# Where the first value products of a head and the wait for a later head's operands stand in TensorE's order

## The chip, the cores and the metric

One core of one Trainium2 chip runs the whole program. The metric is the time of one execution on the device, in microseconds (us). Three runs of the kernel before took 1323.6, 1324.37 and 1325.23 us.

## The reference

The program is one macaron block over x of 4 sequences x 1024 tokens x 128 channels in float32: half a mixture of experts, attention, and half a mixture of experts again.

```
x = x + 0.5 * ffn(layernorm(x))
x = x + attn(layernorm(x))      # 16 heads of 8 channels, rotary q and k
x = x + 0.5 * ffn(layernorm(x))

scores  = einsum('bhqd,bhkd->bhqk', q, k) * SCALE      # 1024 x 1024 per head
weights = softmax(scores, axis=-1)
attn    = einsum('bhqk,bhkd->bhqd', weights, v)
```

The change touches the attention only, between q, k, v and the output projection: 4 x 16 = 64 heads of 1024 queries by 1024 keys.

## The kernel before

Each engine has its own instruction stream, written out by hand. The streams meet in counting semaphores. The attention is a pipeline over the 64 heads, called n here: heads 0 to 3 and 60 to 63 are written out, heads 4 to 59 are a hardware loop of 14 rounds of four heads (u = 0 to 3 in a round).

A head has 16 steps on TensorE, i = 0 to 15 (`head`, line 919). A step i issues one score product K(i) of head n (`key_scores`, line 886: 128 keys by 512 queries, with the row maximum already folded in through three extra rows) and one score product M(i) of head n+2 (`max_scores`, line 855: 128 queries by 512 keys, only for the row maximum). K and M use different halves of the array's rows. I call one such step a pair of score products. After every odd step stands a value product W(kb) (`weigh_values`, line 896): eight short matrix products that weigh 128 keys' values by their exponentials. LAG = 2 sets which one: after steps 1 and 3 it is W(6) and W(7) of the head before, after steps 5, 7, ... 15 it is W(0), W(1), ... W(5) of this head. Before step MT_AT = 7 stands T (`max_transpose`, line 877), a product with 24 columns that turns the maximum of head n+1 round; ScalarE copies it (`mrow_copy`) and a DMA puts it into that head's Q.

What waits for what:

- K(i) needs a free score bank of three (`bank_free`, line 869). K(0) waits for exponential E(14) of the head before, K(1) for its E(15), K(6) for E(3), K(7) for E(5), T for E(4).
- M(2t) waits until VectorE has read pair t-2 (`max_read`, line 863), as there are two places for maximum scores. R(t) is VectorE's reduction of M(2t) and M(2t+1) (line 1235). M(6) waits for R(1).
- M(0) waits besides for the operands of head n+2 (`head_loaded`, line 860). SyncE starts these loads for head n+3 at the start of head n (line 352), once W(7) of head n-1 has been issued and done.
- W(0) waits for its exponentials, for `ot_ready` (line 903) and for `vh_ready` (line 904). `ot_ready` comes from ScalarE's copy O of the output bank of the head before (line 649), which stands in ScalarE's stream right behind E(3).
- ScalarE runs E(0) to E(15) in order (line 661), with O behind E(3) and the copy of T ahead of E(7).

Of the kernel before, what the change touches and what calls it, by code (L numbers as in the profile page):

```python
# [46 lines left out]
NH = B * H  # L47
# [11 lines left out]
PIECE = H * CH // P  # L59
QSLOTS = 4  # L60
LAG = 2
PSLOTS = 8
HALVES = 2 * KB

# [11 lines left out]
def at_least(eng, sem, count):  # L76

    if isinstance(count, int) and count <= 0:
        return
    eng.wait_ge(sem, count)  # L80
# [49 lines left out]
def build(nc, x_in, qkv_w, qkv_b, v_b, out_w, out_b, wr_t, w1_in, w2_t, cos_t, sin_t, out):  # L130
# [4 lines left out]
    with ExitStack() as ctx:  # L135
        def sb(name, shape, dt=F32):
            return ctx.enter_context(nc.sbuf_tensor(name, shape, dt))

        def sem(name):
            return ctx.enter_context(nc.semaphore(name))  # L140
# [59 lines left out]
        K = [K_all[u // 2 * HALF:(u // 2 + 1) * HALF, u % 2, :] for u in range(QSLOTS)]  # L200
        probs = sb("probs", [P, PSLOTS, T])

# [76 lines left out]
        head_loaded = [sem(f"head_loaded{u}") for u in range(QSLOTS)]  # L279
# [257 lines left out]
        def _(sc):  # L537
# [113 lines left out]
            def head(r, u, more=True, first=False):  # L651
                n = QSLOTS * r + u
                for i in range(HALVES):
# [4 lines left out]
                    if j == 0:  # L658

                        at_least(sc, probs_used, KB * (n - 1) + kb + 1)  # L660
                    nc.scalar.activation(probs[:, kb % PSLOTS, j * CH:(j + 1) * CH], score[i],  # L661
                                         ACT.Exp, scale=SCALE).then_inc(probs_ready, 1)
# [20 lines left out]
        def _(pe):  # L683
# [5 lines left out]
            def x_transposes(p, k, rotated, bank=tpsum):  # L689
                pe.wait_ge(xn_ready, p + 1)  # L690

                at_least(pe, rot_ready, 2 * rotated)
                at_least(pe, x_lo_ready, p)
                transposes(xn[:, k, :, :], bank).then_inc(xT_in_psum, 1)
# [30 lines left out]
            def values(c):  # L725

                pe.wait_ge(rot_ready, 2 * c + 2)
                for t in range(TPC):
                    last = nc.tensor.matmul(mpsum_all[:, t * P:(t + 1) * P], x2T[:, t * P:(t + 1) * P], wqkv[:, 4, :],  # L729
                                            start=True, stop=True)  # L730
                last.then_inc(v_in_psum, 1)

            def router(p, k, valued, bank=rpsum):
                pe.wait_ge(xnT_ready, p + 1)

                at_least(pe, v_ready, valued)
                at_least(pe, gap_ready, p)
                if isinstance(p, int) and p == 1:

                    pe.wait_ge(w_lo_ready, E)  # L740
                for t in range(TPC):
                    last = nc.tensor.matmul(bank[:, t, :], xnT[:, k, t * P:(t + 1) * P], wr[:], start=True, stop=True)  # L742
                last.then_inc(logits_in_psum, 1)
# [12 lines left out]
            def out_projection(c, bank=tpsum):  # L756
                pe.wait_ge(attn_ready, c + 1)
                for t in range(TPC):
                    last = nc.tensor.matmul(bank[:, t * P:(t + 1) * P], attn[:, t * P:(t + 1) * P], wo[:], start=True, stop=True)  # L759
                last.then_inc(proj_in_psum, 1)  # L760
# [91 lines left out]
                first_max_scores(t)  # L852
            values(NCH - 1)

            def max_scores(r, u, i):

                t, half = i // 2, i % 2
                n = QSLOTS * r + u
                if i == 0:
                    pe.wait_ge(head_loaded[u], 32 * (r + 1))  # L860
                if half == 0:

                    pe.wait_ge(max_read, KB * n + t - 1)
                last = nc.tensor.matmul(maxps[t % 2][:, half, :], Q[u][0:STACK, t * P:(t + 1) * P],  # L864
                                        K[u][0:STACK, half * CH:(half + 1) * CH], start=True, stop=True)
                if half == 1:
                    last.then_inc(max_in_psum, 1)
# [9 lines left out]
            def max_transpose(r, u, first=False):  # L877

                n = QSLOTS * r + u
                pe.wait_ge(mparts_ready, n + 1)  # L880
                if not first:
                    bank_free(n - 1, MT_AT, True)
                nc.tensor.transpose(mpsum, mparts[:, u % 2, :, :].rearrange("p i t -> p (i t)"),  # L883
                                    identb[:]).then_inc(mT_in_psum, 1)

            def key_scores(r, u, i, row):

                n = QSLOTS * r + u
                kb, j = i // 2, i % 2
                if i == 0:  # L890
                    pe.wait_ge(mrow_loaded[u], 16 * (r + 1))
                bank_free(n, SCORE_PLACE[i], row)
                nc.tensor.matmul(score[i], K[u][0:ROWS, kb * P:(kb + 1) * P],  # L893
                                 Q[u][0:ROWS, j * CH:(j + 1) * CH], start=True, stop=True).then_inc(scores_in_psum, 1)

            def weigh_values(r, u, kb):


                n = QSLOTS * r + u
                pe.wait_ge(probs_ready, HALVES * n + 2 * kb + 2)  # L900
                if kb == 0:

                    at_least(pe, ot_ready, n)
                    pe.wait_ge(vh_ready, n + 1)
                for c in range(QUARTERS):
                    last = nc.tensor.matmul(opsum[VW * c:VW * (c + 1), :], vh[:, u % 2, kb, :],  # L906
                                            probs[:, kb % PSLOTS, c * QW:(c + 1) * QW],
                                            start=(kb == 0), stop=(kb == KB - 1), skip_group_check=True)
                last.then_inc(probs_used, 1)

            pe.wait_ge(max_read, KB)
            for i in range(HALVES):
                if i == MT_AT:
                    max_transpose(0, 0, first=True)
                max_scores(0, 1, i)

            pe.wait_ge(v_ready, NCH)

            def head(r, u, maxes=True, row=True, first=False, early=None):
                for i in range(HALVES):  # L920
                    kb, j = i // 2, i % 2
                    if i == MT_AT and row:
                        max_transpose(r + (u + 1) // QSLOTS, (u + 1) % QSLOTS)
                    key_scores(r, u, i, row)
                    if maxes:
                        max_scores(r + (u + 2) // QSLOTS, (u + 2) % QSLOTS, i)
                    if j == 1 and kb >= LAG:
                        weigh_values(r, u, kb - LAG)
                    elif j == 1 and not first:
                        weigh_values(r + (u - 1) // QSLOTS, (u - 1) % QSLOTS, KB + kb - LAG)  # L930
                    if early == 0 and i == 5:

                        pe.wait_ge(max_read, KB * NH)
                        out_projection(0, early_t)
                    if early == 1 and i == 3:
                        x_transposes(NCH, 0, 0, early_t)
                    if early == 1 and i == 9:
                        router(NCH, 0, 0, early_r)

            for u in range(QSLOTS):  # L940
                head(0, u, first=(u == 0))
            with pe.Fori(1, NH // QSLOTS - 1) as r:
                for u in range(QSLOTS):
                    head(r, u)
            for u in range(QSLOTS):
                head(NH // QSLOTS - 1, u, maxes=u < 2, row=u < 3, early=u - 2)
            for kb in range(KB - LAG, KB):
                weigh_values(NH // QSLOTS - 1, QSLOTS - 1, kb)
            pe.wait_ge(ot_ready, NH)
# [375 lines left out]
```

## Time and profile before

| what | value |
|---|---|
| median of three runs | 1324.37 us |
| the profiled execution | 1324.05 us, its span 1322.1 us |
| attention, heads 0 to 63 | about 385 to 1021 us of the span |
| TensorE busy | 1269.0 us (96%) |
| VectorE busy | 1112.9 us (84%) |
| ScalarE busy | 809.9 us (61%) |
| granted TensorE clock, mean of the span | 0.984 |

The span is from the first to the last instruction; the 1.95 us between it and the execution's time lie around it. Busy shares are means over stages with different limits, so the argument below reads one head of the loop instruction by instruction. The start of a TensorE instruction in a timeline is recorded; its end is modelled, so distances between starts are used.

### The profile page before, as it was taken

To read this page: it belongs to the slowest core of one execution; us is meant where nothing else is said; L and a number is where in the kernel's file an instruction comes from. 1 tells how busy PE (TensorE), PEld (TensorE's weight loads), DVE (VectorE), ACT (ScalarE), POOL (GpSimd) and SP (SyncE) were. 2 spreads that over 40 slices of the span, in tenths; PEclk is the share of its full clock that TensorE was granted. 3 is DMA by queue.
4 is the path that set the end of the run, shared out by engine and by line. 5 is a ranking of instruction groups with operands and counts; after the bars stand their busy time and mean duration, and the time that the engine had idled before them with its cause. 6 is when DMAs were issued, how large, how long until landed. Compare 5 with 4: busy or idle time off the path is not lost.

```text
span 1322.1 us, 32042 instructions
## 1 busy us (share of the span) xinstructions
PE 1269.0 (96%) x10240; PEld 616.0 (47%) x10240; DVE 1112.9 (84%) x2306; ACT 809.9 (61%) x1540; POOL 143.4 (11%) x450
## 2 busy tenths in 40 slices
PE   6999999999889999999999999999999999999998
PEld 3666666667522222222222222222223776767776
DVE  7888867887789999999999999999994787777775
ACT  4433333333239999999999999999997333333332
POOL 1020122111221111111111111111110000000000
PEclk9999999999969999999999999999998999999999
DMA  7010111011211100101101011010010100000000
GB/s 207 1 30 19 49 49 48 12 37 49 67 54 32 42 31 31 40 30 39 32 30 40 31 31 40 30 40 31 31 54 14 35 27 27 27 27 21 13 9 9
DMA packets 52265, 48.49 MB, mean 37 GB/s; under 512 B 10080, under 2 KB 44768, under 8 KB 52192
## 3 DMA queue, kind: packets, MB, share of 16 engines
q1 hardware_dynamic: 52192, 47.61, 12.4%
q8 instruction: 34, 0.56, 0.2%
q14 instruction: 39, 0.32, 0.1%
HBM read 23.86 MB, written 23.33 MB: 36 GB/s over the span
## 4 chain that ended last, share of the span: by engine, by line
PE 89%; DVE 5%; issue 4%; ACT 1%; DVEq 0%; DMA 0%; ACTq 0%; SPq 0%
PE ps L765 23%; PE ps L906 22%; PE ps L893 21%; PE ps L752 16%; PE ps L722 2%; PE ps L864 1%; PE ps L742 1%; DVE X L1092 1%; PE ps L686 1%; PE ps L883 1%; PE ps L729 1%; ACT probs L661 1%; DVE mx L1235 1%; DVE act L1080 1%; PE ps L759 1%
## 5 line engine op out<-in xcount | busy, mean ns | idle before, releaser
L1235 DVE TENSOR_REDUCE mx<-ps 128x1 f32<-128x1024 f32 x512 | 591.7, 1217 | 35.9 <-PE ps L864 30.0
L661 ACT ACTIVATE probs<-ps 128x512 f32<-128x512 f32 x1024 | 562.4, 597 | 60.7 <-PE ps L893 42.6
L590 ACT ACTIVATE sg<-ps,unscale 128x512 f32<-128x512 f32 x256 | 173.8, 687 | 307.2 <-PE ps L765 283.0
L906 PE MATMUL ps<-probs,vh 128*32 128x256 f32 x4096 | 330.7, 395 | 16.9 <-issue 11.5
L893 PE MATMUL ps<-Q,K 51*128 51x512 bf16 x1024 | 333.3, 386 | 0.9 <-ACT probs L661 0.5
L864 PE MATMUL ps<-K,Q 48*128 48x512 bf16 x1008 | 327.1, 389 | 2.9 <-DVE mx L1235 2.5
L752 PEld LDWEIGHTS ps<-w,act 128*128 128x128 f32 x2048 | 247.9, 192 | 17.1
L752 PE MATMUL ps<-w,act 128*128 128x128 f32 x2048 | 249.0, 275 | 0.0
L1080 DVE SCALAR_TENSOR_TENSOR act<-ps,unscale,sg 128x512 f32<-128x512 f32 x256 | 183.3, 744 | 60.0 <-ACT sg L590 19.2
L765 PE MATMUL ps<-x_hi,w_hi 128*128 128x512 f16 x512 | 195.6, 382 | 9.9 <-DVE act L1080 6.4
L1092 DVE SCALAR_TENSOR_TENSOR X<-ps,rw,X 128x128 f32<-128x128 f32 (+1 forms) x512 | 143.9, 343 | 62.4 <-PE ps L752 61.8
L765 PE MATMUL ps<-x_lo,w_hi 128*128 128x512 f16 x512 | 195.4, 382 | 0.0
L765 PE MATMUL ps<-x_hi,w_lo 128*128 128x512 f16 x512 | 195.3, 381 | 0.0
L893 PEld LDWEIGHTS ps<-Q,K 51*128 51x128 bf16 x1024 | 72.7, 93 | 235.4 <-ACT probs L661 227.5
L906 PEld LDWEIGHTS ps<-probs,vh 128*32 128x32 f32 x4096 | 82.8, 108 | 207.8 <-ACT probs L661 162.1
L765 PEld LDWEIGHTS ps<-x_hi,w_hi 128*128 128x128 f16 x512 | 51.8, 101 | 63.9 <-DVE act L1080 12.0
L765 PEld LDWEIGHTS ps<-x_hi,w_lo 128*128 128x128 f16 x512 | 50.4, 98 | 61.4 <-issue 1.7
L864 PEld LDWEIGHTS ps<-K,Q 48*128 48x128 bf16 x1008 | 71.7, 93 | 14.0 <-DVE mx L1235 9.4
L765 PEld LDWEIGHTS ps<-x_lo,w_hi 128*128 128x128 f16 x512 | 50.3, 98 | 49.6 <-issue 5.5
L502 POOL TENSOR_SCALAR negm<-mx 128x8 f32<-128x8 f32 x64 | 15.1, 236 | 493.0 <-DVE mx L1235 493.0
L481 POOL TENSOR_TENSOR qf<-rot 128x512 f32<-128x512 f32 x16 | 20.4, 1274 | 258.9 <-DVE rot L1124 258.9
L580 ACT ACTIVATE tanh_gap<-gap 128x4 f32<-128x4 f32 x16 | 3.3, 204 | 52.5 <-DVE gap L1049 52.5
(84 smaller groups left out, 608.9 us busy)
## 6 DMA issues: line engine op xcount, KB each, us to landing
o_parts<-ot SPq DMA_DIRECT2D x64, 128.0 KB, 1.9
q_stack<-parts SPq DMA_DIRECT2D x48, 128.0 KB, 2.3
k_stack<-parts SPq DMA_DIRECT2D x48, 128.0 KB, 2.3
Q<-q_stack SPq DMA_DIRECT2D x64, 96.0 KB, 2.3
K<-k_stack SPq DMA_DIRECT2D x64, 96.0 KB, 2.3
probs<-w_in SPq DMA_DIRECT2D x8, 256.0 KB, 4.3
att<-o_parts SPq DMA_DIRECT2D x16, 128.0 KB, 2.6
rden<-rdens SPq DMA_DIRECT2D x16, 128.0 KB, 2.5
```

Source lines behind the costliest of these rows:

```text
L481: nc.gpsimd.tensor_tensor(qf[:, w, :], rot[:, w, 0, :], rot[:, w, 1, :], ALU.add).then_inc(rot_sum, 1)
L590: nc.scalar.activation(sg[:, j, :], hid[2 * j], ACT.Silu, scale=unscale[:, e, 2 + j:3 + j]).then_inc(silu_done, 1)
L661: nc.scalar.activation(probs[:, kb % PSLOTS, j * CH:(j + 1) * CH], score[i], ACT.Exp, scale=SCALE).then_inc(probs_ready, 1)
L722: last = nc.tensor.matmul(bank, wqkv[:, 2 * w + i, :], x2T[:], start=True, stop=True)
L752: last = nc.tensor.matmul(ypsum[s][:, t, :], act[:, s, j, t * P:(t + 1) * P], w2[:, e, j, :], start=(j == 0), stop=(j == 1))
L765: last = nc.tensor.matmul(bank, w[:, e, at:at + P], x[:, k, :], start=(n == 0), stop=(n == 2))
L864: last = nc.tensor.matmul(maxps[t % 2][:, half, :], Q[u][0:STACK, t * P:(t + 1) * P], K[u][0:STACK, half * CH:(half + 1) * CH], start=True ...
L893: nc.tensor.matmul(score[i], K[u][0:ROWS, kb * P:(kb + 1) * P], Q[u][0:ROWS, j * CH:(j + 1) * CH], start=True, stop=True).then_inc(scores_ ...
L906: last = nc.tensor.matmul(opsum[VW * c:VW * (c + 1), :], vh[:, u % 2, kb, :], probs[:, kb % PSLOTS, c * QW:(c + 1) * QW], start=(kb == 0), ...
L1080: nc.vector.scalar_tensor_tensor(out=act[:, e % 2, j, :], in0=hid[2 * j + 1], scalar=unscale[:, e, j:j + 1], in1=sg[:, j, :], op0=ALU.mult ...
L1092: last = nc.vector.scalar_tensor_tensor(out=xt, in0=ypsum[e % 2][:, t, :], scalar=rw[:, k, t, e:e + 1], in1=xt, op0=ALU.mult, op1=ALU.add)
L1235: nc.vector.tensor_reduce(mx[:, u % 2, t:t + 1], pair.rearrange("p a b -> p (a b)"), AX_X, ALU.max).then_inc(max_read, 1)
```

## The change

Three things change, all in TensorE's stream.

W(0) is issued after step 6 and no longer after step 5. T, which stays ahead of step 7, then stands right behind it. All other value products stay where they were.

The wait for `head_loaded` leaves M(0). It stands ahead of K(15) of the head before (`operands`, called in `head` at the last step); for the first heads it stands ahead of the maximum scores of head 1 and ahead of head 0.

The order of the out projection (line 934) and of W(0) in head 62 is turned round by the first point.

```diff
+FIRST_VALUES = 2 * LAG + 2
...
+            def operands(r, u):
+                pe.wait_ge(head_loaded[u], 32 * (r + 1))
+
             def max_scores(r, u, i):
...
-                if i == 0:
-                    pe.wait_ge(head_loaded[u], 32 * (r + 1))
...
             pe.wait_ge(max_read, KB)
+            pe.wait_ge(head_loaded[1], 32)
...
-            def head(r, u, maxes=True, row=True, first=False, early=None):
+            operands(0, 2)
+
+            def head(r, u, maxes=True, row=True, first=False, early=None, ahead=True):
                 for i in range(HALVES):
                     kb, j = i // 2, i % 2
+                    if i == HALVES - 1 and ahead:
+                        operands(r + (u + 3) // QSLOTS, (u + 3) % QSLOTS)
...
-                    if j == 1 and kb >= LAG:
+                    if i == FIRST_VALUES:
+                        weigh_values(r, u, 0)
+                    elif j == 1 and kb > LAG:
                         weigh_values(r, u, kb - LAG)
-                    elif j == 1 and not first:
+                    elif j == 1 and kb < LAG and not first:
                         weigh_values(r + (u - 1) // QSLOTS, (u - 1) % QSLOTS, KB + kb - LAG)
...
-                head(NH // QSLOTS - 1, u, maxes=u < 2, row=u < 3, early=u - 2)
+                head(NH // QSLOTS - 1, u, maxes=u < 2, row=u < 3, early=u - 2, ahead=u < 1)
```

## Rows read from the trace of the kernel before

**Rows 1.** The page's costliest groups: busy us, mean ns, idle before, releaser.

```profile
L1235 DVE TENSOR_REDUCE mx<-ps 128x1 f32<-128x1024 f32 x512 | 591.7, 1217 | 35.9 <-PE ps L864 30.0
L906 PE MATMUL ps<-probs,vh 128*32 128x256 f32 x4096 | 330.7, 395 | 16.9 <-issue 11.5
```

**Rows 2.** Busy time of each engine while the loop runs, PE first.

```profile
427.00:975.00 548.00, 531.88 (x5435) 147.72 (x5432) 516.99 (x449) 503.41 (x1009) 70.38 (x336) 1.00 0.11 34
```

**Rows 3.** Timeline of PE (start, us, instruction): K(0) of heads 4 and 60.

```profile
427.11 0.39 PE L893 MATMUL ps<-Q,K 51*128 51x512 bf16 x1
...
975.45 0.37 PE L893 MATMUL ps<-Q,K 51*128 51x512 bf16 x1
```

**Rows 4.** Timeline of PE, steps 13 and 14 of head 21, and W(5) in halves.

```profile
601.34 0.38 PE L893 MATMUL ps<-Q,K 51*128 51x512 bf16 x1
...
601.65 0.64 PE L906 MATMUL ps<-probs,vh 128*32 128x256 f32 x8
602.23 0.39 PE L893 MATMUL ps<-Q,K 51*128 51x512 bf16 x1
...
602.76 0.42 PE L906 MATMUL ps<-probs,vh 128*32 128x256 f32 x4
...
603.00 0.40 PE L906 MATMUL ps<-probs,vh 128*32 128x256 f32 x4
```

**Rows 5.** Timeline of PE, start of head 22: K(0), M(0), K(1).

```profile
603.38 0.39 PE L893 MATMUL ps<-Q,K 51*128 51x512 bf16 x1
603.58 0.38 PE L864 MATMUL ps<-K,Q 48*128 48x512 bf16 x1
603.87 0.39 PE L893 MATMUL ps<-Q,K 51*128 51x512 bf16 x1
```

**Rows 6.** Timeline of ACT: E(15) of head 21.

```profile
603.22 0.59 ACT L661 ACTIVATE probs<-ps 128x512 f32<-128x512 f32 x1
```

**Rows 7.** Timeline of ACT, head 22: E(3), the copy O, E(5).

```profile
605.75 0.59 ACT L661 ACTIVATE probs<-ps 128x512 f32<-128x512 f32 x1
...
606.23 0.39 ACT L649 ACTIVATE ot<-ps 128x256 f32<-128x256 f32 x1
...
606.97 0.63 ACT L661 ACTIVATE probs<-ps 128x512 f32<-128x512 f32 x1
```

**Rows 8.** Timeline of PE, head 22: K(5), W(0), T, K(7).

```profile
606.09 0.38 PE L893 MATMUL ps<-Q,K 51*128 51x512 bf16 x1
...
606.72 0.64 PE L906 MATMUL ps<-probs,vh 128*32 128x256 f32 x8 [0.25 <-issue]
...
607.61 0.23 PE L883 MATMUL ps<-identb,mparts 128*24 128x128 bf16 x1
607.77 0.39 PE L893 MATMUL ps<-Q,K 51*128 51x512 bf16 x1
```

**Rows 9.** Timeline of DVE, head 22: R(1).

```profile
605.47 1.21 DVE L1235 TENSOR_REDUCE mx<-ps 128x1 f32<-128x1024 f32 x1
```

**Rows 10.** Timeline of PE, head 28, first of its round: K(5), W(0).

```profile
664.77 0.38 PE L893 MATMUL ps<-Q,K 51*128 51x512 bf16 x1
...
665.53 0.64 PE L906 MATMUL ps<-probs,vh 128*32 128x256 f32 x8 [0.39 <-ACT ot L649]
```

**Rows 11.** Timelines of DVE and PE ahead of head 0: an R, an M that waits.

```profile
376.80 1.22 DVE L1235 TENSOR_REDUCE mx<-ps 128x1 f32<-128x1024 f32 x1
...
378.08 0.60 PE L864 MATMUL ps<-K,Q 48*128 48x512 bf16 x1 [1.86 <-DVE mx L1235]
```

**Rows 12.** Timeline of PE in the second mixture: two kinds of full-array products.

```profile
1100.44 0.38 PE L765 MATMUL ps<-x_hi,w_lo 128*128 128x512 f16 x1
1100.65 0.61 PE L752 MATMUL ps<-w,act 128*128 128x128 f32 x4
```

**Rows 13.** The operand load: its issue in head 22, and the page's median landing.

```profile
606.60 0.37 SPq L352 DMA_DIRECT2D K<-k_stack  x1
...
K<-k_stack SPq DMA_DIRECT2D x64, 96.0 KB, 2.3
```

## The prediction

> **What bounds the kernel now.** I read the page first, then the busy times of the loop, then the timeline of one head. VectorE's reductions cost most [rows 1] and sat idle only 35.9 us in all, nearly always for a maximum score. So two engines are close to full. While the loop runs, TensorE is busy 531.9 of 548 us, VectorE 517.0, ScalarE 503.4 [rows 2]. A head takes (975.45 - 427.11) / 56 = 9.79 us [rows 3]. The chain of waits follows TensorE, so the timeline of its starts decides.
>
> The unit is two pairs of score products and a value product. The last pair before a value product costs 0.31 us, from 601.34 to 601.65. The value product costs 0.58, from 601.65 to 602.23 (0.57 by the unrounded starts). Its two halves start 0.24 apart [rows 4]. With 0.22 for the other pair a unit is 1.11 us, and eight of them are 8.86. The remaining 0.9 us of a head are three places. At the head's start K(1) comes 0.49 after K(0) where 0.22 would do [rows 5]. W(0) comes 0.63 after K(5) where 0.31 would do [rows 8]. T puts 0.25 between K(6) and K(7). The change touches all three.
>
> **Part 1, the wait for operands.** It is one register calculation and one wait. Today M(0) starts 0.20 after K(0), where K and M otherwise start together [rows 5], so this looks like the cause of the loss at the head's start. It isn't: E(15) of the head before ends at 603.22 + 0.59 = 603.81 [rows 6], and K(1) starts at 603.87, one semaphore later. K(1) may not write its bank sooner, whatever M(0) does. E(15) hangs on E(14) and that on K(14) at 602.23 [rows 4]. So I cost the gain at zero; the cover is E(15), and without it the gain could be 0.49 - 0.22 = 0.27 us a head.
>
> In its new place the wait stands ahead of K(15), M(15) and W(5), and K(0) is queued behind these. Its condition is old by then: the K load is issued at 606.60 and lands some 2.3 us later, at 608.9 [rows 13]; K(15) of this head stands a pair and a value product (0.31 + 0.61) ahead of the next K(0), and so at about 603.38 + 9.79 - 0.92 = 612.2. Slack is over 3 us. The issue cost is bounded below by 0 and above by the 0.20 us that M(0) shows today. Even 0.20 is swallowed: K(1) has 0.27 us in hand against its predecessors on TensorE, and E(15) starts behind E(14), not behind K(15). I take 0. No DMA is moved by it, and SyncE's, GpSimd's and VectorE's orders are untouched.
>
> **Part 2, W(0) one pair later.** Removed: the stall at W(0). O runs from 606.23 to 606.62, behind E(3) [rows 7], and W(0) starts at 606.72 [rows 8], against 606.40 with no wait. That is 0.32 us of idle TensorE in each head. Moving K(6) and M(6) ahead would fill it. K(6) can: E(3) ends at 605.75 + 0.59 = 606.34 [rows 7], so K(6) starts at about 606.40.
>
> What is late next is M(6). It needs R(1), which ends at 605.47 + 1.21 = 606.68 [rows 9]. From an R's end to the waiting M I read 378.08 - 378.02 = 0.06 us [rows 11]. So M(6) can't start before 606.74, about when W(0) starts today. TensorE takes instructions in order: W(0), T, K(7), M(7), then VectorE's R(3), all queue behind M(6). O is past by then. The stall changes its owner from ScalarE's copy to VectorE's reduction, and W(0) moves from 606.72 to 606.74 + 0.31 [rows 4] = 607.05.
>
> Then T. Today it follows K(6) and sits between two changes of the array's shape, each with a gap of about 0.1 us: a 512-column product takes 0.21 us where products of one shape follow each other [rows 12], but 0.31 ahead of a value product [rows 4]. Now it follows W(0). No row of before shows that pair. The upper bound is the 0.57 of a value product before a score product [rows 4]. The lower bound is what lets K(7) start: K(7) needs E(5), which ends at 606.97 + 0.63 = 607.60 [rows 7], so K(7) >= 607.65. I take 0.48, twice the distance of W's halves [rows 4]: T uses all 128 rows and 24 columns, W all rows and 32, and the halves, equal in shape, follow with no such gap.
>
> The Trainium skill, TensorEngine Tiling (Array Packing), Key Properties, says that changing the tiling mode drains the engine while changing only the tile doesn't. That agrees with the gaps above and would give my value if T counts as a 32-column tile.
>
> The row of like shapes [rows 12] shows 0.21 us, hence no time for loading weights between two products on the same rows. The Trainium skill, TensorE: Matmul & The Clock Gate, Part 3, says that a weight load overlaps running products only when the row group differs; by that rule T's load would stand bare behind W(0) and the sum would be that of the first rival. The trace speaks against the rule there.
>
> The sum for one head:
>
> - now K(7) at 607.77 [rows 8];
> - then 606.74 + 0.31 + 0.48 + 0.16 (T to K(7), 607.77 - 607.61 [rows 8]) = 607.69. Gain 0.08 us.
> - In the first head of each round W(0) comes 0.76 after K(5) [rows 10], not 0.63. These 0.13 are extra time at W(0) behind O. M(6) now waits longer than that, so they disappear under its wait. Gain 0.08 + 0.13 = 0.21, with rounding 0.22.
>
> After K(7) all is as before: R(3) comes earlier by the same time, VectorE is busy 517.0 / 56 = 9.23 us of a 9.7 us head [rows 2], and E(14), E(15) hang on K(14), so K(1)'s stall travels along unchanged.
>
> Over the loop: 42 x 0.08 + 14 x 0.22 = 6.4 us. The eight heads outside give about nothing: without loop arithmetic W(0) waits less there, so the exchange is even; head 62 may gain 0.2 by having the projection before W(0). Total 6.6 us. The profiled execution would go from 1324.05 to 1317.5, which stands 0.3 under the median; against the median the forecast is **1317.8 us**. With K(7) at its floor the gain is 42 x 0.12 + 14 x 0.26 = 8.7, so 1315.7.
>
> **The rivals.**
>
> *T pays for the change anyway.* With 0.57 behind W(0), K(7) comes at 607.78. 42 heads lose 0.01, 14 gain 0.12: 1.3 us, with head 62 1.5, so **1322.9 us**, no measurable change. For it: every change of work around W shows the gap [rows 4]. Against it: W's own halves don't.
>
> *Slower: M(6) holds up the instruction stream.* W(0) carries two waits of its own besides that for its exponentials. If they are worked off only once M(6) has gone, W(0) follows not at 0.31 but with the extra 0.13 us that the first head of a round shows at this place [rows 10]. It decides if the issue work behind M(6) exceeds the 0.31 us that M(6) covers, and then the waits of T add theirs, so that T comes at 0.57. K(7) is at 607.78 + 0.14 = 607.92: 42 x 0.15 = 6.3 us lost, the first heads of rounds even: **1330.7 us**. For it: the M(0) that follows K(0) by 0.20 behind such a wait [rows 5]. Against it: weight loads and products stream ahead of running ones elsewhere, and there the register work is covered by a product of 0.3 us.
>
> *The head's start opens after all.* If K(1) hangs on M(0) and not on E(15), 56 x 0.27 = 15 us more go: **1302.7 us**. Against it stand the 0.06 us between E(15)'s end and K(1) [rows 5, 6], which is the usual semaphore time.
>
> *The change doesn't do what it says* would mean that O still is last at W(0). O ends at 606.62 and M(6) can't go before 606.74, so this would take R(1) coming 0.1 us sooner; the time would be that of the floor.
>
> **How the numbers follow.** Forecast with its floor 0.58, T's gap 0.22, held-up stream 0.13, head's start 0.04, the rest 0.03, split over both sides. A measurement of this kernel tells about 0.2%, 2.65 us, from no change. The forecast and the head's start are faster: 0.63 with a part of the rest; T's gap is the same; the held-up stream is slower. The range takes in the floor (1315.7, with a little for reading) and T's gap with an issue cost of 0.03 us a head on top (1324.6), 0.8 of the chance: 1315.4 to 1324.6.
>
> **What the changed profile would show.** K(6) starts ahead of M(6) by some 0.3 us in each loop head, and M(6) is put down to VectorE. W(0) is no longer released by ScalarE's copy. W(0) to T is 0.48 (right) or 0.57 (first rival). M(6) to W(0) is 0.31 (right) or 0.4 and more (second). M(0) starts within 0.1 of K(0), yet K(1) stays 0.49 behind K(0). All four heads of a round take 9.7 us, and ScalarE's E(6) comes 0.3 us sooner with nobody waiting for it. The prediction is wrong above all if W(0) to T is misjudged, since 0.1 us there is 5.6 us of the result, or if R(1) moves against the head's start.

## The result and the profile after

The changed kernel takes 1314.55 us, the median of six runs from 1312.99 to 1315.37; the kernel before, run beside it, 1324.16 (1322.73 to 1325.71). The ratio is 0.9929, its 95% interval 0.9919 to 0.9939. The change is faster by 9.6 us; 6.6 were forecast, and the result lies 0.85 us below the lower end of the range.

| what | before | after |
|---|---|---|
| the profiled execution, us | 1324.05 | 1314.48 |
| its span, us | 1322.1 | 1312.4 |
| loop, K(0) of head 4 to K(0) of head 60 | 548.34 | 540.57 |
| head 0, K(0) to K(0) of head 1 | 13.31 | 11.94 |
| TensorE / VectorE / ScalarE busy, us | 1269.0 / 1112.9 / 809.9 | 1275.5 / 1111.3 / 803.4 |
| granted clock, mean of the span | 0.984 | 0.985 |

The page's costliest groups after the change, to be set against [rows 1]:

```profile
L1243 DVE TENSOR_REDUCE mx<-ps 128x1 f32<-128x1024 f32 x512 | 591.4, 1217 | 27.3 <-PE ps L866 21.3
L908 PE MATMUL ps<-probs,vh 128*32 128x256 f32 x4096 | 329.3, 394 | 0.0
```

VectorE idles 8.6 us less, and no idle time of TensorE is left before the value products (16.9 before). The busy times while the loop runs, PE first, against [rows 2], and K(0) of heads 4 and 60 in the timeline, against [rows 3]:

```profile
425.30:965.90 540.60, 540.00 (x5436) 151.96 (x5433) 517.26 (x449) 496.32 (x1009) 69.81 (x336) 1.00 0.11 35
```

```profile
425.34 0.39 PE L895 MATMUL ps<-Q,K 51*128 51x512 bf16 x1
...
965.91 0.37 PE L895 MATMUL ps<-Q,K 51*128 51x512 bf16 x1
```

TensorE is now busy in all but 0.6 us of the loop. That busy figure flatters: a product's end is modelled, and one whose successor waits looks long. The starts tell more. The timeline of TensorE in head 22 after the change, from K(0) to K(7), with the steps that hold nothing new left out, against [rows 5, 8]:

```profile
599.01 0.39 PE L895 MATMUL ps<-Q,K 51*128 51x512 bf16 x1
599.11 0.38 PE L866 MATMUL ps<-K,Q 48*128 48x512 bf16 x1
599.50 0.39 PE L895 MATMUL ps<-Q,K 51*128 51x512 bf16 x1
...
601.72 0.38 PE L895 MATMUL ps<-Q,K 51*128 51x512 bf16 x1
...
602.03 0.39 PE L895 MATMUL ps<-Q,K 51*128 51x512 bf16 x1
602.37 0.39 PE L866 MATMUL ps<-K,Q 48*128 48x512 bf16 x1
602.68 0.64 PE L908 MATMUL ps<-probs,vh 128*32 128x256 f32 x8
603.14 0.22 PE L885 MATMUL ps<-identb,mparts 128*24 128x128 bf16 x1
603.29 0.39 PE L895 MATMUL ps<-Q,K 51*128 51x512 bf16 x1
```

Read it by differences. M(0) follows K(0) by 0.10 and no longer by 0.20 (before, the lag was 0.19 to 0.20 in the first and third head of a round and 0.10 in the other two); K(1) still comes 0.49 behind K(0). K(6) starts 0.31 behind K(5), M(6) 0.34 behind K(6), W(0) 0.31 behind M(6), T 0.46 behind W(0), K(7) 0.15 behind T. K(7) is 4.28 behind K(0), where it was 4.39. What M(6) and K(7) wait for stands in the timelines of VectorE, the reduction R(1), and of ScalarE, the copy O and the exponential E(5), against [rows 7, 9]:

```profile
601.10 1.22 DVE L1243 TENSOR_REDUCE mx<-ps 128x1 f32<-128x1024 f32 x1
```

```profile
601.86 0.39 ACT L650 ACTIVATE ot<-ps 128x256 f32<-128x256 f32 x1
...
602.60 0.64 ACT L662 ACTIVATE probs<-ps 128x512 f32<-128x512 f32 x1
```

R(1) ends at 602.32 and M(6) starts 0.05 later. O ends at 602.25, long before W(0). E(5) ends at 603.24 and K(7) starts 0.05 later. The list of waits over the loop says the same of the maximum scores, a wait that the list of before does not have:

```profile
PEld ps L866 <- DVE mx L1243: 13.7, 56, 0.3
DVE mx L1243 <- PE ps L866: 17.6, 58, 0.3
```

56 times, once a head, TensorE waited for a reduction, 13.7 / 56 = 0.24 us each. In the chain of work that ended last (start, length, what), other pairs of score products are one step of 0.32 or 0.21 us; in head 22, K(6) and M(6) are two steps of 0.32 and 0.33:

```profile
602.10 0.32 PE ps L895
602.42 0.33 PE ps L866
602.75 0.57 PE ps L908 x8
603.32 0.04 PE ps L885
```

Over heads 8 to 55 a head takes 9.65 us in all four places of a round, where it took 9.76 in three and 9.89 in the first. 42 x 0.107 + 14 x 0.243 = 7.9 us, the 7.8 of the table within rounding. Of the 9.6 us in the profiled executions 7.8 lie in the loop and 1.4 in head 0. The other 0.4 stand ahead of head 0, whose K(0) starts at 384.68 and not at 385.06, where the order of products is the same; over all the profiles of this study that start lies anywhere from 383.8 to 386.7.

### The profile page after: what moved, and what is told of

The parts are those of the page before. It is cut to its first block, busy times and chain, and to the rows that moved or that the text cites. A ratio compares the mean times of both kernels' runs of the same rounds, so it can differ in the third digit from the quotient of the medians.

```text
span 1312.4 us, 32041 instructions
## 1 busy us (share of the span) xinstructions
PE 1275.5 (97%) x10240; PEld 620.6 (47%) x10240; DVE 1111.3 (85%) x2306; ACT 803.4 (61%) x1540; POOL 142.6 (11%) x450
## 3 DMA queue, kind: packets, MB, share of 16 engines
q1 hardware_dynamic: 52192, 47.61, 12.6%
## 4 chain that ended last, share of the span: by engine, by line
PE 91%; DVE 6%; issue 2%; ACT 0%; DMA 0%; DVEq 0%; SPq 0%; ACTq 0%
PE ps L766 23%; PE ps L908 22%; PE ps L895 22%; PE ps L753 16%; PE ps L866 2%; PE ps L723 2%; DVE mx L1243 2%; PE ps L743 1%; DVE X L1100 1%; PE ps L687 1%; PE ps L730 1%; PE ps L760 1%; DVE act L1088 1%; DMA w<-w_t 0%; PE ps L705 0%
## 5 line engine op out<-in xcount | busy, mean ns | idle before, releaser
L895 PE MATMUL ps<-Q,K 51*128 51x512 bf16 x1024 | 328.6, 386 | 1.4 <-ACT probs L662 0.7
L753 PEld LDWEIGHTS ps<-w,act 128*128 128x128 f32 x2048 | 247.9, 192 | 17.1
L766 PEld LDWEIGHTS ps<-x_hi,w_hi 128*128 128x128 f16 x512 | 51.8, 101 | 63.0 <-DVE act L1088 11.9
```

The costliest lines, as they stand in the source:

```text
L753: last = nc.tensor.matmul(ypsum[s][:, t, :], act[:, s, j, t * P:(t + 1) * P], w2[:, e, j, :], start=(j == 0), stop=(j == 1))
L766: last = nc.tensor.matmul(bank, w[:, e, at:at + P], x[:, k, :], start=(n == 0), stop=(n == 2))
```

## The experiments

Each time stands beside runs of the kernel before on the same chip. Times within a head are counted from its K(0) and are medians over heads 8 to 55.

### The two parts apart

**e1_operands_only** has the moved operand wait alone. From the changed kernel:

```diff
-                    if i == FIRST_VALUES:
-                        weigh_values(r, u, 0)
-                    elif j == 1 and kb > LAG:
+                    if j == 1 and kb >= LAG:
                         weigh_values(r, u, kb - LAG)
-                    elif j == 1 and kb < LAG and not first:
+                    elif j == 1 and not first:
```

> Only the wait for the operands is moved; W(0) stays behind step 5. Theory (the wait was covered by E(15), it gains nothing): 1324.2 us, no difference beyond 0.2%; M(0) starts within 0.1 us of K(0), K(1) still 0.49 behind K(0), W(0) still 0.63 behind K(5), a loop of 548 us from K(0) of head 4 to K(0) of head 60. Rival (the 3 us that I had not forecast come from this part): 1321 us, and K(0) or K(1) come sooner. Rival (the head's start hangs on this wait): 1309 us.

Measured: 1323.34 us against 1323.44, ratio 0.9998 (0.9989 to 1.0007). Head 22's K(0), M(0) and K(1), then K(5) and W(0) in TensorE's timeline:

```profile
602.67 0.39 PE L895 MATMUL ps<-Q,K 51*128 51x512 bf16 x1
602.76 0.38 PE L866 MATMUL ps<-K,Q 48*128 48x512 bf16 x1
603.15 0.39 PE L895 MATMUL ps<-Q,K 51*128 51x512 bf16 x1
...
605.38 0.38 PE L895 MATMUL ps<-Q,K 51*128 51x512 bf16 x1
...
606.01 0.42 PE L908 MATMUL ps<-probs,vh 128*32 128x256 f32 x4 [0.25 <-issue]
```

M(0) comes 0.1 us sooner and K(1) stays at 0.49; the loop takes 548.34 us, to the hundredth what it took before. W(0) is still 0.63 behind K(5). The wait's place is worth nothing, in its old place and in its new one.

**e2_values_only** leaves the operand wait at M(0) and moves W(0):

```diff
+FIRST_VALUES = 2 * LAG + 2
...
-                    if j == 1 and kb >= LAG:
+                    if i == FIRST_VALUES:
+                        weigh_values(r, u, 0)
+                    elif j == 1 and kb > LAG:
                         weigh_values(r, u, kb - LAG)
-                    elif j == 1 and not first:
+                    elif j == 1 and kb < LAG and not first:
```

> Only W(0) is moved behind step 6; the wait for the operands stays ahead of M(0). Theory (this part alone carries the result): 1314.5 us, loop of 540.6 us, K(7) 4.28 behind K(0) in all four heads of a round, M(0) again 0.2 behind K(0) in two of four. Rival (the parts need each other, or the operands' wait carries 3 us): 1317.8 us or more.

Measured: 1314.65 us, ratio 0.9934 (0.9921 to 0.9948); loop 540.44 us, head 0 12.02. M(0) lags by 0.20 again in two heads of four, as expected. This is the whole gain.

### The gap in front of T

**e3_wide_turn** makes T a product with 128 columns in place of 24 by padding its input with zeros; result, place and waits stay.

```diff
-        mparts = sb("mparts", [P, 2, PARTS, KB], BF16)
+        mparts = sb("mparts", [P, 2, 16, KB], BF16)
...
+        mpsum_out = ps[0:16 * KB, MT_BANK, 0:P // 2].bitcast(BF16)
...
+            seq.then(nc.gpsimd.memset(mparts[:], 0.0))
...
-                nc.tensor.transpose(mpsum, mparts[:, u % 2, :, :].rearrange("p i t -> p (i t)"),
+                nc.tensor.transpose(mpsum_out, mparts[:, u % 2, :, :].rearrange("p i t -> p (i t)"),
```

> As the changed kernel, but T has 128 columns and not 24: the tile with the maximum's parts is filled up with zeros, so that T no longer has the shape of the value products' 32 columns. Theory (T is quick behind W(0) because both have one shape): W(0) to T grows from 0.46 to 0.57 us, K(7) comes 4.39 to 4.40 behind K(0), 0.11 us x 56 heads = 6 us more than the changed kernel, 1320.7 us. Rival (any product on all rows follows W(0) like this; K(7) hangs on E(5) alone): 1314.6 us, W(0) to T 0.46.

Measured: 1321.12 us, ratio 0.9988 (0.9978 to 0.9998). TensorE's timeline from M(6) to K(7) of a loop head whose K(0) is at 601.74:

```profile
605.10 0.39 PE L868 MATMUL ps<-K,Q 48*128 48x512 bf16 x1
605.42 0.64 PE L910 MATMUL ps<-probs,vh 128*32 128x256 f32 x8
605.99 0.23 PE L887 MATMUL ps<-identb,mparts 128*128 128x128 bf16 x1
606.15 0.39 PE L897 MATMUL ps<-Q,K 51*128 51x512 bf16 x1
```

M(6) and W(0) stand where they stood. W(0) to T is 0.57 and no longer 0.46, and K(7) comes 0.12 later; the loop takes 547.52 us, 7.0 more. So the first rival was no phantom: 0.12 us per head in one gap is the difference between a gain of 9.6 us and one of 2.3. T takes 128 streamed columns in both versions; the width of its weights differs, and with it the number of rows that it writes. The record of its weight load lasts 0.10 us in place of 0.09, so the length of the load isn't the 0.12; weights and output were widened together, and the run doesn't part these two. The Trainium skill, TensorEngine Tiling (Array Packing), Key Properties, says that a change of tiling mode drains the engine and a change of tile does not. The run agrees, if T's 24 columns count as a tile like W's 32, though no edit here tests the change of mode by itself; the gap is 0.12 us here.

### What holds M(6)

**e4_max_first** issues M(1) ahead of K(1), so that VectorE starts its first reduction sooner.

```diff
+                    if maxes and i == 1:
+                        max_scores(r + (u + 2) // QSLOTS, (u + 2) % QSLOTS, i)
                     key_scores(r, u, i, row)
-                    if maxes:
+                    if maxes and i != 1:
```

> As the changed kernel, but in step 1 M(1) is issued ahead of K(1), so it no longer waits for E(15), and R(0), R(1) and M(6) come 0.17 us sooner. Two bounds are claimed to meet at K(7) at 4.28 behind K(0): M(6) behind R(1), and E(5). Theory (both bind): M(6) moves from 3.36 to 3.19 behind K(0), W(0) and T with it, K(7) stays at 4.28 because of E(5): 1314.6 us, no change. Rival (only the chain over R(1) binds): K(7) at 4.11, 0.17 x 56 = 9.5 us less, 1305 us.

Measured: 1313.42 us, ratio 0.9923 (0.9908 to 0.9938); loop 539.90, 0.7 under the changed kernel's. K(7) at 4.275 is again E(5)'s end, 4.220, and 0.055: E(5) holds it, as expected. M(6) was to come at 3.19 and comes at 3.33. Where that failed is seen in the timelines of TensorE (K(0), M(0) with M(1), M(3), M(6)) and of VectorE (R(0), R(1)):

```profile
599.19 0.39 PE L895 MATMUL ps<-Q,K 51*128 51x512 bf16 x1
599.29 0.60 PE L866 MATMUL ps<-K,Q 48*128 48x512 bf16 x2
...
600.80 0.38 PE L866 MATMUL ps<-K,Q 48*128 48x512 bf16 x1
...
602.53 0.39 PE L866 MATMUL ps<-K,Q 48*128 48x512 bf16 x1
```

```profile
599.95 1.22 DVE L1245 TENSOR_REDUCE mx<-ps 128x1 f32<-128x1024 f32 x1
...
601.24 1.23 DVE L1245 TENSOR_REDUCE mx<-ps 128x1 f32<-128x1024 f32 x1
```

M(1) is issued 0.22 behind M(0), at 599.51, and R(0) starts 0.44 behind it. R(0) ends at 601.17 at the latest, and R(1) starts at 601.24, which is 0.44 behind M(3). R(1) is now held by its own scores, not by R(0), so that a still sooner R(0) moves nothing. In the changed kernel R(0) held it: R(1) starts 1.14 behind R(0) there, and VectorE's reductions never start less than 1.13 apart.

**e6_reduce_ahead** takes from R(0) besides a wait for the maximum's parts and puts it ahead of the head's last two reductions.

```diff
-                at_least(dve, mparts_ready, n - 1)
                 for t in range(KB):
+                    if t == KB - 2 and more:
+                        at_least(dve, mparts_ready, n)
...
```

> As the kernel with M(1) ahead of K(1), and besides VectorE's wait for the split maxima of an earlier head stands ahead of R(6) of the head before and not ahead of R(0). Theory (two bounds meet at K(7)): R(0) starts at 0.77 instead of 0.92 behind K(0), M(6) at 3.19 instead of 3.33, T at 3.95, but K(7) stays at 4.28, 0.055 behind the end of E(5): 1313.4 us, no change. Rival (K(7) only follows from M(6)): K(7) at 4.11, 1304 us.

Measured: 1312.62 us, ratio 0.9914 (0.9898 to 0.9931). The time is about what was expected (1313.4). R(0) starts at 0.76, as it did in e4 already, R(1) at 2.05 and M(6) at 3.33 and not at 3.19, the loop takes 539.90 us: the wait that was moved held nothing. The 0.8 us between the two medians are not in the loop.

**e7_copy_on_vector** adds to that the copy O on VectorE in place of ScalarE (for heads 0 to 60), to bring E(5) forward.

```diff
-                    if i == 3 and not first:
+                    if i == 3 and late:
                         o_copy(r + (u - 1) // QSLOTS, (u - 1) % QSLOTS)
...
                     tile_max(n, u, t, maxps[t % 2])
+                    if t == 1 and copies:
+                        o_copy(r + (u - 3) // QSLOTS, (u - 3) % QSLOTS)
```

> As the kernel before in this list, and besides the copy O is made by VectorE, behind R(1), for heads 0 to 60. Theory: without O ahead of them E(4) and E(5) come 0.26 us sooner and no longer hold K(7); O now ends about 0.4 us behind R(1), at 3.5, W(0) starts at 3.6, T at 4.06 and K(7) at 4.21: 1309.7 us. If E(5) is no bound at all the time stays at 1313.4.

Measured: 1314.6 us, ratio 0.9933 (0.9917 to 0.995); loop 542.72. K(7) stays at 4.285 in three heads of four and comes at 4.44 in a round's first, but E(5) ends at 4.07, 0.21 ahead of the earlier one. So E(5) is off the path, and the copy has come on it: VectorE makes it from 3.19 to 3.60, W(0) moves from 3.67 to 3.71 and in a round's first head to 3.84. The forecast of 1309.7 counted one bound taken away and not the next one behind it. In the changed kernel K(7) has two last conditions that fall together: E(5) ends at 4.229, and 0.055 later is 4.284; T starts at 4.130, and 0.154 later is 4.284.

### The head's start

K(1) waits for E(15) because K(1)'s bank is the one that E(15) reads. The next kernels deal the three banks round from head to head (17 places in a head in place of 18), so that K(1) needs E(14) and K(0) needs E(13). The bank then depends on n modulo 3, and the loop body holds twelve heads in place of four, on TensorE and on ScalarE.

**e5_rotate:**

```diff
-PLACES = 18
+PLACES = 17
...
+        def bank_of(v, place):
+            return (PLACES * v + place) % SCORE_BANKS
...
-            with pe.Fori(1, NH // QSLOTS - 1) as r:
-                for u in range(QSLOTS):
-                    head(r, u)
+            with pe.Fori(1, 13, 3) as r:
+                for n in range(3 * QSLOTS):
+                    head(r + n // QSLOTS, n % QSLOTS, (QSLOTS + n) % 3)
+            for n in range(13 * QSLOTS, NH - QSLOTS):
+                head(n // QSLOTS, n % QSLOTS, n % 3)
```

> As the changed kernel, but the three score banks are dealt round from head to head (17 places a head and none skipped, the loop written out for 12 heads), so that K(1) no longer needs the bank of E(15) but that of E(14), three products back. Theory (K(1) waited for E(15) and nothing else; behind it VectorE binds, since R(0) starts 0.92 behind K(0), right after R(7) has ended): K(1) at 0.23 behind K(0) instead of 0.49, M(6) still at 3.33, K(7) at 4.26: 1313 us, 1 to 2 us less than the changed kernel. Rival (the 0.26 us at the head's start are TensorE's own and come off the head): 1300 us.

**e8_rotate_reduce_ahead** adds e6's change of VectorE's wait:

> Banks dealt round and VectorE's wait ahead of R(6), O on ScalarE, M(1) behind K(1). Theory: with K(1) at 0.23 both chains to K(7) start 0.26 us sooner (E(2), E(3), O, E(4), E(5)) or 0.17 sooner (R(0), R(1), M(6), W(0), T): K(7) at 4.09 instead of 4.28, 0.19 x 56 = 11 us less than the changed kernel, 1303.5 us. Rival (the larger loop body of 12 heads costs instruction fetches, or VectorE at 9.4 us a head binds): 1308 us or more.

Measured: e5 1313.89 us (ratio 0.9926, 0.9904 to 0.9948), e8 1312.97 (0.9926, 0.9901 to 0.9951). The head did nearly what e5's rival said, 0.20 of the 0.26 us: K(1) at 0.226, M(6) at 3.208, K(7) at 4.132, a head 9.45 us. These times are the same in both kernels to 0.001, so e6's change does nothing here either. Yet the loop takes 544.15 us in e5 and 543.21 in e8. Two heads in each of three places are far too long: in e8 heads 15 and 16 take 12.30 and 10.61, 27 and 28 take 12.69 and 11.90, 39 and 40 take 12.43 and 10.78, which is 4.0 + 5.7 + 4.3 = 14.0 us over 9.45 each (15.0 in e5). These are the loop's back edges, where it jumps back to its start. Busy times at the first one of e5 (in the last three columns the granted clock, the DMA share and GB/s), and TensorE's first product behind it:

```profile
539.70:552.40 12.70, 9.58 (x79) 2.39 (x77) 7.46 (x7) 7.35 (x16) 1.26 (x6) 0.73 0.10 30
```

```profile
542.91 0.60 PE L899 MATMUL ps<-Q,K 51*128 51x512 bf16 x1 [3.12 <-issue]
```

TensorE stands idle for 3.12 us with nothing waited for ("issue"); the trace's record of the branch lasts 3.76 us (0.21 to 0.23 in the loops of four heads). The granted clock falls to its lower level, 1.2 GHz, at 541.8, when TensorE has stood idle for 2.0 us, and stays there for 6.8 us (6.8 and 3.4 at the other two). So e5 measured two things at once, and its median near the first theory's 1313 is chance. The next two kernels part them.

**e10_rotate_flat** writes heads 4 to 59 of e5 out, with no loop, here TensorE's lines; ScalarE's are changed alike:

```diff
-            with pe.Fori(1, 13, 3) as r:
-                for n in range(3 * QSLOTS):
-                    head(r + n // QSLOTS, n % QSLOTS, (QSLOTS + n) % 3)
-            for n in range(13 * QSLOTS, NH - QSLOTS):
+            for n in range(QSLOTS, NH - QSLOTS):
                 head(n // QSLOTS, n % QSLOTS, n % 3)
```

> Banks dealt round as two kernels earlier, W(0) behind step 6, and the heads of TensorE and ScalarE written out instead of looped. Theory (the dealt-round loop lost 8 us at its three back edges of 12 heads, where TensorE stood still and its clock fell): no stall and no half clock between the heads, 9.33 to 9.45 us a head: 1297 to 1304 us. Rival (instruction fetch stalls come with the size of the stream, not with the jump): stalls of 3 to 4 us stay, 1310 us or more.

**e11_rotate_hint** keeps e5's loop of twelve heads and marks its back edge with a prefetch hint, on ScalarE too:

```diff
-            with pe.Fori(1, 13, 3) as r:
+            with nc.Fori(1, 13, 3, engines=OrderedEngineSet([pe.engine]), hint_back_edge=True) as r:
```

> The same dealt-round banks in the loop of 12 heads, with a hint of the jump back armed at the top of each pass. Theory: the first head of each pass no longer stalls, 9.45 us a head throughout, 1304 us. Rival (the hint reaches too short for a body of this size): 1313 us as without it.

Measured: e10 1299.83 us (ratio 0.9822, 0.9807 to 0.9837), e11 1299.43 (0.9817, 0.9802 to 0.9832), loops 529.2 and 529.98 us. No stop is left. In e11 the heads behind a jump take 9.45 us like the others, and the branch record lasts 0.34 to 0.38 us; its 0.78 us over e10 stand in the third head of each pass (0.12 to 0.14, of which the next gives 0.05 back) and at head 54, behind the loop (0.5). TensorE's timeline of a head of e10: K(0), K(1), K(6), M(6), W(0), T, K(7):

```profile
594.72 0.39 PE L896 MATMUL ps<-Q,K 51*128 51x512 bf16 x1
...
594.94 0.38 PE L896 MATMUL ps<-Q,K 51*128 51x512 bf16 x1
...
597.38 0.39 PE L896 MATMUL ps<-Q,K 51*128 51x512 bf16 x1
597.92 0.39 PE L867 MATMUL ps<-K,Q 48*128 48x512 bf16 x1 [0.15 <-DVE mx L1243]
598.24 0.64 PE L909 MATMUL ps<-probs,vh 128*32 128x256 f32 x8
598.70 0.22 PE L886 MATMUL ps<-identb,mparts 128*24 128x128 bf16 x1
598.85 0.39 PE L896 MATMUL ps<-Q,K 51*128 51x512 bf16 x1
```

K(1) is 0.22 behind K(0), and 0.18 ahead of E(15)'s end, which shows by an edit that E(15) was what held it: of TensorE's order and waits at the head's start only the banks were changed, and e5, with a loop, has the same 0.226. Of the 0.26 us won there 0.11 are given back at M(6), which now waits 0.54 behind K(6) and is put down to the reduction; another 0.05 are won at the next K(0), which no longer waits for E(14) and stands 0.57 behind W(5) and not 0.62. That makes 0.20 a head.

### A better order

**e15_turn_first** uses that wait. On e10, W(0) and T stand between K(6) and M(6):

```diff
-                    if i == MT_AT and row:
-                        max_transpose(r + (u + 1) // QSLOTS, (u + 1) % QSLOTS, v)
                     key_scores(r, u, v, i, row)
+                    if i == FIRST_VALUES:
+                        weigh_values(r, u, 0)
+                        if row:
+                            max_transpose(r + (u + 1) // QSLOTS, (u + 1) % QSLOTS, v)
...
```

> As the written-out kernel with banks dealt round, but in step 6 the order is K(6), W(0), T, M(6): the wait for R(1) no longer stands ahead of W(0) and T. Theory (behind M(6) W(0) and T were queued; now O sets W(0) at 2.99, T follows at 3.51, held by E(4), M(6) at 3.67, and K(7) comes with E(5)'s end at 3.93 instead of 4.13): 0.15 to 0.2 us a head less, 1289 to 1292 us. Rival (VectorE, which then stands still by 0.2 us a head only, or K(7) and M(7) in separate turns take it back): 1298 us or more.

Measured: **1290.59 us**, ratio 0.9745 (0.9731 to 0.9759), the best of the study, 24 us under the changed kernel. TensorE's timeline from K(6) to K(7), K(0) at 592.46, and the busy times of the loop:

```profile
595.13 0.39 PE L896 MATMUL ps<-Q,K 51*128 51x512 bf16 x1
595.45 0.64 PE L909 MATMUL ps<-probs,vh 128*32 128x256 f32 x8
595.99 0.22 PE L886 MATMUL ps<-identb,mparts 128*24 128x128 bf16 x1
596.14 0.39 PE L867 MATMUL ps<-K,Q 48*128 48x512 bf16 x1
596.39 0.39 PE L896 MATMUL ps<-Q,K 51*128 51x512 bf16 x1
```

```profile
426.05:943.77 517.72, 517.72 (x5436) 138.23 (x5433) 512.05 (x449) 495.36 (x1009) 69.10 (x336) 1.00 0.13 38
```

M(6) stands 0.15 behind T and shows no stall. A head takes 9.245 us. VectorE is busy 512.05 of 517.72 us. Its reductions start 1.13 us apart where nothing holds them, so eight of them need 9.05 us of the 9.245, and by this estimate 11 us are left in this stage before they bound it. W(0) to T is 0.54 here and not 0.46. T's last condition, E(4), ends 0.145 ahead of it, where K(7) follows E(5)'s end by 0.055, and the list of waits names no releaser; what holds T by the rest is open. It costs little, since E(5) holds K(7), as expected.

### Head 0

Head 0 is written out, outside the loop, and took 13.31 us, now 11.94. During it the clock is granted in part at its lower level. Busy times and clock of the same 3.5 us, before, after, and in e12, which follows (0.4 us later, as it starts later):

```profile
392.50:396.00 3.50, 3.50 (x24) 0.53 (x20) 2.02 (x2) 2.17 (x4) 0.00 (x0) 0.50 0.01 2
```

```profile
392.50:396.00 3.50, 3.50 (x40) 0.87 (x38) 3.19 (x3) 3.27 (x7) 0.00 (x0) 0.99 0.00 0
```

```profile
392.90:396.40 3.50, 3.50 (x24) 0.54 (x20) 2.00 (x2) 2.17 (x4) 0.00 (x0) 0.50 0.01 2
```

24 products where the changed kernel has 40, at 0.50 against 0.99: before, the half clock (1.2 GHz) ends 11.1 us behind K(0) of head 0, in the changed kernel's profile 7.9 us behind it.

**e9_first_head_only** has the new order in head 0 alone, **e12_not_first_head** everywhere but there; **e13_first_head_again** and **e14_changed_again** are a second trace each of e9's kernel and of the changed kernel.

```diff
e9:
-                    if i == FIRST_VALUES:
+                    if i == (FIRST_VALUES if first else FIRST_VALUES - 1):
e12:
-                    if i == FIRST_VALUES:
+                    if i == (FIRST_VALUES - 1 if first else FIRST_VALUES):
```

> As the changed kernel, but W(0) and T stand in their new order in head 0 alone; heads 1 to 63 have W(0) behind step 5 again. Theory (the 1.4 us that head 0 lost in the changed kernel belong to the change: TensorE's half clock ends 3.4 us sooner there): head 0 takes 11.9 to 12.0 us and not 13.3, the half clock lasts 20.5 us and not 23.9, the loop is 548.3 us as before: 1322 us, 1.4 less than the kernel before. Rival (the clock's stretches differ from run to run and have nothing to do with the order): 13.3 us in some runs of either kernel, 1323.4 us.

> The complement of the kernel with the new order in head 0 alone: head 0 has W(0) behind step 5, all other heads behind step 6. Theory (the loop's part is 7.8 us and stands by itself; head 0's shorter half clock belongs to head 0's order): loop 540.5 us, head 0 again 13.3 us with its half clock ending 11.1 us behind its K(0): 1316 us. Rival (head 0's clock has nothing to do with the order): head 0 at 12 us here too, 1314.6 us.

> The kernel with the new order in head 0 alone once more, for a second trace. Theory: head 0 of 11.9 to 12.0 us, half clock ending 7.6 to 8.1 us behind K(0) of head 0, as in the changed kernel. Rival (chance): 13.3 us, ending at 11.1.

> The changed kernel once more, for a second trace. Theory: head 0 of 11.9 to 12.0 us, loop 540.6 us. Rival (chance): head 0 of 13.3 us.

| kernel | median us | ratio (95%) | head 0, us | half clock ends behind K(0) |
|---|---|---|---|---|
| e9 | 1319.56 | 0.9966 (0.9952 to 0.9979) | 12.74 | 9.7 |
| e12 | 1313.43 | 0.9927 (0.9913 to 0.9941) | 13.29 | 11.1 |
| e13, one run | 1326.51 | | 12.68 | 9.6 |
| e14, one run | 1316.66 | | 12.75 | 9.75 |

The outcomes were not all as expected. e12's head 0 and loop (540.44 us) came as its theory said, but its median is 2.6 us below the 1316. In e9, e13 and e14 head 0 took neither the 11.9 to 12.0 of the theory nor the 13.3 of the rival, and e9's median is 2.4 us below the 1322.

The stretches at the lower level, which the granted clock of each trace shows, sort the profiles. In most of them there is one of 6.8 us that starts 26 us ahead of head 0 and a second one from about 13 us ahead of it on. There the second lasts 23.9 us and head 0 takes 13.3 with the old order (before, e1, e12), and 20.5 us and 11.8 to 12.0 with the new one (after, e2, e3, e4, e6, e7, e8, e10, e11). e12 differs from the changed kernel in the order in head 0 alone. So the order in head 0 does move the end of the half clock there, and it is worth 1.4 us. e15, which has a third order, W(0) and T ahead of M(6), has 23.9 and 13.26 again.

In e5, e9, e13 and e14 the first stretch lasts 13.7 us and the second starts 7 to 8 us ahead of head 0 and lasts 17.1; head 0 takes 12.6 to 12.75. The difference is there before head 0 begins, and two traces of one kernel (after, e14) show either, so the edits don't set it. No profile has this pattern with the old order, so these runs don't show what the order is worth in it.

They also show a limit of this reckoning. e12 lacks head 0's gain and is yet no slower than the changed kernel; in its profile a half-clock stretch of 6.8 us that stands at the end of the attention in the changed kernel is missing. e9's runs fall apart into five from 1318.27 to 1320.99 at a mean clock of 0.988 to 0.990 and two of 1324.32 and 1325.24 at 0.985; its profile is one of the latter, has the loop and the clock of before, and has a stretch of 10.2 us at that end. The stretch at the end is there in before, e1, after, e2, e4, e6, e9, e13, e14 and e15, and absent in e3, e5, e7, e8, e10, e11 and e12. Without it the part of the span behind K(0) of head 60 is shorter by two to three microseconds (346.5 us in the changed kernel, 343.5 in e12), and no edit here was found that governs it. Medians that lie closer than that, such as those of e4, e6 and e7, are better compared by their loops.

## Why the prediction was off by three microseconds

- **What bounds the kernel: right.** Reading starts in TensorE's timeline found the three places, and nearly all that the study won within a head came from them. A fourth was in its rows and not read: K(0) stands 603.38 - 602.76 = 0.62 behind W(5) [rows 4, 5] where 0.57 would do, held by E(14), and the change of banks took these 0.05 off.
- **Part 1 costs and gains nothing: right.** e1 is even to 0.1 us. The lag of 0.20 that it read from head 22 is there in two heads of four only. That M(0)'s lag is not what holds K(1) was argued from 0.06 us between E(15) and K(1); e10 shows it by changing the bank. The cover named for it, E(15), is real: with it gone K(1) comes 0.26 us sooner (0.27 was the estimate).
- **The stall changes its owner: right, and to the hundredth.** M(6) was put at 3.36 behind K(0) and is at 3.36, W(0) at 3.67, and the releaser is R(1), as the list of waits shows. W(0) follows M(6) at 0.31. The extra 0.13 of a round's first head vanished as worked out: all four heads take 9.65.
- **T's gap: right in kind, mis-sized by 0.02 us; a term of the sum that failed.** The step took 0.48 for W(0) to T, twice the distance of W's halves. Measured: 0.456. W's second half does start 0.24 behind the first, but T follows the second half by only 0.215; the distance of two halves was not the distance of a half and T. K(7) is at 4.284 and not at 4.31, so that T by its gap and E(5) by its end let it start at the same time. 56 x 0.026 = 1.4 us, so that the loop gave 7.8 in place of 6.4. e3 confirms the mechanism: with a wide T the rival's 0.57 and 1321 us come true (its forecast was 1322.9).
- **"The eight heads outside give about nothing": this step failed.** Head 0 gave 1.4 us in the profiled run. The prediction looked for waits at W(0) there and not at the clock, which stood at its lower level for 23.9 us, up to 11.1 us behind head 0's K(0). A row of before would have shown that level, as the window above does, though not that the order moves its end. Without these 1.4 us the result would have been within the range. Of the other heads 62 gave 0.37 (0.2 was the estimate) and 60 took 0.17 back.
- **The range.** Its lower end was the floor of the loop (1315.7) with 0.3 for reading, and nothing for the clock outside the loop. That left out head 0 (1.4 us) and the stretch at the attention's end (two to three us either way). With these the low end would have been near 1312.
- **The rivals.** T's gap: refuted for 24 columns, true for 128. Held-up stream: refuted by M(6) to W(0) at 0.31. The head's start opening with the moved wait: refuted by e1; e10 shows what an open start is worth, 0.20 us a head net of the 0.27 that this rival counted. That O stays last: refuted by O's end at 602.25 against M(6) at 602.37.

In the 9.6 us of the profiled executions, 7.8 are the loop and are shown; 1.4 are head 0 and are shown to hang on the order there, in the pattern of the clock that these two profiles have; the remaining 0.4 stand ahead of head 0, where the start varies by more than that from profile to profile. How often either pattern of the clock ahead of head 0, and the stretch at the attention's end, stood in the runs without a trace is open.

## What to carry to other kernels

When a product is moved ahead of a stall, price the new neighbours by the shape of their weights as well as by their waits: here 24 or 128 columns behind a 32-column product decided between 9.6 and 2.3 us. Write down the next two conditions behind the stall that is taken away (here R(1) for M(6), E(5) for K(7)), since their distance, not the stall's length, is the gain; the best order came from putting ready work into the place of the new stall. And look at the granted clock in every stretch that runs outside the loop before saying that nothing happens there.

## What the hardware showed beyond this

- The back edge of a loop body of twelve heads stopped TensorE for 3.12 us (the branch record 3.76) with up to 6.8 us of half clock from within that stop on, 4 to 6 us lost each time; the body of four heads showed neither (branch records of 0.21 to 0.23 us). Written out, or with a prefetch hint on the back edge, both are gone (e10, e11).
- [rows 12] and the W(0) to T of 0.46 leave no time for T's weights to be loaded bare between two products that use all rows. In head 22 after the change the record of T's load starts 0.24 behind W(0)'s start at 602.68 and ends 0.13 ahead of T's start:

```profile
602.92 0.09 PEld L885 LDWEIGHTS ps<-identb,mparts 128*24 128x24 bf16 x1
```

The Trainium skill, TensorE: Matmul & The Clock Gate, Part 3, says that a weight load overlaps running products only when the row group differs; the measurement decides against it here.
- A register calculation and a wait ahead of M(0) delayed it by 0.1 us in two heads of four (0.20 before, 0.10 in e1) and not at all in the other two, yet cost the kernel nothing, as something else holds the next product.
- VectorE's reductions of 1.22 us start 1.13 us apart when nothing holds them (medians over the loop of e10), so that their records overlap by 0.09 us and the busy time is not the time they need.
